# Attention scores and row maxima as products over one head's rows, and k and q placed early in an item

## The reference

```python
xn = _layernorm(x, axis=-1)
...
qkv = (x @ w_qkv.T + b_qkv).reshape(b, n, 3, H, D).transpose(2, 0, 3, 1, 4)
q, k, v = (qkv[0], qkv[1], qkv[2])
q = jax.nn.elu(q) + 1.0
k = jax.nn.elu(k) + 1.0
q = _apply_rope(q, sin, cos)
k = _apply_rope(k, sin, cos)
attn = jnp.einsum('bhnd,bhmd->bhnm', q, k) * scale
attn = jax.nn.softmax(attn, axis=-1)
attn_out = jnp.einsum('bhnm,bhmd->bhnd', attn, v)
...
x = x + s * g
```

## Time and profile before

| | us |
|---|---|
| three runs | 1500.83, 1501.16, 1502.19 |
| median | 1501.16 |
| span of the profiled execution | 1499.6 |
| PE busy | 1385.7 (92%) |
| VectorE busy | 1244.3 (83%) |
| ScalarE busy | 862.0 (57%) |
| GpSimd busy | 371.7 (25%) |
| 1024 score products (L1070), mean of one | 0.428 |
| 1024 maxima products (L1093), mean of one | 0.409 |
| 1024 reductions (L1217), mean of one | 0.685 |
| 1024 exponentials (L1154), mean of one | 0.600 |

### The profile page before, as it was taken

How to read it: one execution, slowest core, us unless ns; L and a number is a source line. 1 busy time by engine, 2 the same in 40 slices (tenths; PEclk the granted TensorE clock), 3 DMA queues, 4 the chain that set the end, 5 groups by cost and what they waited for, 6 DMA issues and landing times.

```text
span 1499.6 us, 25714 instructions
## 1 busy us (share of the span) xinstructions
PE 1385.7 (92%) x6898; PEld 875.8 (58%) x6898; DVE 1244.3 (83%) x2163; ACT 862.0 (57%) x1551; POOL 371.7 (25%) x455
## 2 busy tenths in 40 slices
PE   4599997999899894699999999999999999999998
PEld 4477775877677673455555555555555555555553
DVE  7799997999799995788887888888888888888881
ACT  5444453444345442057666766766766676676767
POOL 5012221221222315420330331232133033033000
PEclk8699999999999997599999999999999999999999
DMA  5211211112021111111011011101101101101100
GB/s 169 60 28 29 59 41 43 35 35 49 22 56 38 46 43 33 39 44 47 4 45 47 5 44 45 23 26 45 44 4 45 46 3 45 46 8 42 46 8 5
DMA packets 91576, 57.90 MB, mean 39 GB/s; under 512 B 38368, under 2 KB 85344, under 8 KB 90976
## 3 DMA queue, kind: packets, MB, share of 16 engines
q1 hardware_dynamic: 91488, 56.97, 15.1%
HBM read 29.04 MB, written 4.33 MB: 22 GB/s over the span
## 4 chain that ended last, share of the span: by engine, by line
PE 57%; DVE 2%; issue 1%; DMA 0%; ACT 0%; SPq 0%; ACTq 0%; POOLq 0%; POOL 0%; DVEq 0%
PE pa L1070 19%; PE pa L1082 17%; PE pa L1093 16%; PE pa L1116 2%; PE pa L1126 2%; PE pa L1121 1%; DVE neg_half L1217 1%; DVE feat L819 0%; ACT prob L1154 0%; PE pa L1110 0%; DVE w_cur L809 0%; DMA q_mask<-q_raw 0%; DMA w_all<-in_wqkv 0%; SPq L954 0%; SPq L965 0%
## 5 line engine op out<-in xcount | busy, mean ns | idle before, releaser
L1217 DVE TENSOR_REDUCE neg_half<-pa 128x1 f32<-128x512 f32 x1024 | 645.6, 685 | 128.3 <-PE pa L1093 115.2
L1154 ACT ACTIVATE prob<-pa 128x512 f32<-128x512 f32 x1024 | 545.1, 600 | 233.3 <-PE pa L1070 207.4
L1070 PE MATMUL pa<-q_sh,k_mask 128*128 128x512 f32 x1024 | 433.2, 428 | 4.9 <-ACT prob L1154 4.6
L1093 PE MATMUL pa<-k_raw,q_mask 128*128 128x512 f32 x1024 | 412.6, 409 | 1.3 <-DVE neg_half L1217 0.7
L559 ACT ACTIVATE hidden<-ps,b 128x512 f32<-128x512 f32 x320 | 220.5, 689 | 279.8 <-DVE hid_lo L591 187.9
L1070 PEld LDWEIGHTS pa<-q_sh,k_mask 128*128 128x128 f32 x1024 | 191.4, 188 | 240.7 <-ACT prob L1154 188.6
L591 DVE TENSOR_TENSOR hid_lo<-hidden,hid_hi 128x512 fp32r<-128x512 f32 x320 | 274.1, 857 | 10.9
L1082 PE MATMUL pa<-prob,v_st 128*32 128x512 f32 x2048 | 272.7, 604 | 1.1 <-ACT prob L1154 0.7
L1093 PEld LDWEIGHTS pa<-k_raw,q_mask 128*128 128x128 f32 x1024 | 196.2, 192 | 45.4 <-DVE neg_half L1217 18.0
L652 POOL TENSOR_TENSOR acc<-acc,gated 128x512 f32<-128x512 f32 x64 | 85.2, 1332 | 388.0 <-DVE gated L606 387.3
L589 DVE CAST hid_hi<-hidden 128x512 fp32r<-128x512 f32 x320 | 148.3, 463 | 35.8 <-ACT hidden L559 21.3
(11 more groups left out here) (136 smaller groups left out, 1065.4 us busy)
## 6 DMA issues: line engine op xcount, KB each, us to landing
gates<-gate_scratch SPq DMA_DIRECT2D x64, 256.0 KB, 4.9
k_mask<-k_raw SPq DMA_DIRECT2D x64, 128.0 KB, 2.6
q_sh<-q_raw SPq DMA_DIRECT2D x16, 512.0 KB, 3.1
q_mask<-q_raw SPq DMA_DIRECT2D x64, 96.0 KB
w_in<-in_w SPq DMA_DIRECT2D x4, 1280.0 KB, 6.2
x_q<-in_x SPq DMA_DIRECT2D x4, 512.0 KB, 7.2
x_c<-in_x SPq DMA_DIRECT2D x8, 256.0 KB, 5.5
rest_scratch<-rest SPq DMA_DIRECT2D x8, 256.0 KB, 5.4
```

What stands on the lines that cost most here:

```text
L1070: nc.tensor.matmul(score_bank(n, par, s)[:, :], k_mask[par][:, j, kt * P:(kt + 1) * P], q_sh[par][:, qh * CH:(qh + 1) * CH], start=True, s ...
L1093: nc.tensor.matmul(m_ps[(k + par) % MB][:, :], q_mask[par][:, j, qt * P:(qt + 1) * P], k_raw[par][:, kh * CH:(kh + 1) * CH], start=True, s ...
L1154: nc.scalar.activation(prob[s // J % 2][:, j, :], score_bank(n, par, s)[:, :], ACT.Exp, scale=SCALE)\
L1217: nc.vector.tensor_reduce(out=neg_half[par][:, qt, j, kh:kh + 1], in_=m_ps[(k + par) % MB][:, :], axis=AX.X, op=ALU.max, negate=True)\
```

## The change

- `k_mask`, `q_mask`, `q_sh`, their clearing, their DMAs and their semaphores are gone.
- A score product now takes rows 32j to 32j+26 of `k_raw` and `q_raw`, a maxima product rows 32j to 32j+24. The shift rows are placed into `q_raw`.
- The maxima go through the heads in another order (`part_of`), one step on, so that score and maxima of one slot have heads two apart.
- k and q of item n+1 are transposed in item n, in slots 3, 5, 9 and 11, instead of those of item n+2 in slots 47 to 61.
- The first eight rounds have a bank each.

```diff
-    AT_SHIFT1, AT_QKV, AT_K, AT_Q, AT_SHIFT0, AT_LAST_OUT = 23, (13, 17), (47, 51), (57, 61), 54, 7
+    AT_SHIFT1, AT_QKV, AT_K, AT_Q, AT_SHIFT0, AT_LAST_OUT = 23, (13, 17), (3, 5), (9, 11), 54, 7
...
+        def part_of(k):
+
+            return k // (2 * J), (k + 1) % J, k // J % 2
+
...
-            return psum[r] if type(n) is int and n == -2 else shared_ps
+            return psum[r] if type(r) is int and r < len(psum) else shared_ps
...
-            if f:
+            if m:
                 out += [(AT_K[h], "k", h) for h in range(2)] + [(AT_Q[h], "q", h) for h in range(2)]
...
-                    sp.dma_start(q_sh[par][rows, h * CH:(h + 1) * CH].bitcast(F32),
+                    sp.dma_start(q_raw[par][rows, h * CH:(h + 1) * CH].bitcast(F32),
...
-            for mask in (q_mask[0], k_mask[0]):
-                nc.gpsimd.memset(mask[:, :, :].bitcast(F32), 0.0).then_inc(mask_ok, 1)
...
-                nc.tensor.matmul(score_bank(n, par, s)[:, :], k_mask[par][:, j, kt * P:(kt + 1) * P],
-                                 q_sh[par][:, qh * CH:(qh + 1) * CH], start=True, stop=True).then_inc(s_full, 1)
+                rows = slice(j * ROWS, j * ROWS + SHIFT + 2)
+                nc.tensor.matmul(score_bank(n, par, s)[:, :], k_raw[par][rows, kt * P:(kt + 1) * P],
+                                 q_raw[par][rows, qh * CH:(qh + 1) * CH], start=True, stop=True).then_inc(s_full, 1)
...
-                nc.tensor.matmul(m_ps[(k + par) % MB][:, :], q_mask[par][:, j, qt * P:(qt + 1) * P],
-                                 k_raw[par][:, kh * CH:(kh + 1) * CH], start=True, stop=True).then_inc(max_full, 1)
+                rows = slice(j * ROWS, j * ROWS + SHIFT)
+                nc.tensor.matmul(m_ps[(k + par) % MB][:, :], q_raw[par][rows, qt * P:(qt + 1) * P],
+                                 k_raw[par][rows, kh * CH:(kh + 1) * CH], start=True, stop=True).then_inc(max_full, 1)
...
-                        if kind == "k" and has(n)[0]:
-
-                            act.wait_ge(max_full, HALVES * (n + 1))
-                            act.wait_ge(kmask_in[par], 16 * J * (n // 2 + 1))
-                        if kind == "q" and has(n)[0]:
-
-                            act.wait_ge(qmask_in[par], 16 * J * (n // 2 + 1))
-                            act.wait_ge(q_sh_in[par], 16 * (n // 2 + 1))
+                        if after(n):
+
+                            act.wait_ge(s_full, SLOTS * n)
```

More of the change, by code:

```diff
@@ L721, in attention @@
         q_raw = [sb(f"q_raw{i}", [P, T], F32R) for i in range(2)]
-        k_mask = [sb(f"k_mask{i}", [P, J, T], F32R) for i in range(2)]
-        q_mask = [sb(f"q_mask{i}", [P, J, T], F32R) for i in range(2)]
-        q_sh = [sb(f"q_sh{i}", [P, T], F32R) for i in range(2)]
         shift = [sb(f"shift{i}", [P, J, 2, CT], F32R) for i in range(2)]
@@ L756, in attention @@
         raw_ok = sem("a_raw_ok")
-        qmask_in = [sem(f"a_qmask_in{i}") for i in range(2)]
-        kmask_in = [sem(f"a_kmask_in{i}") for i in range(2)]
         max_full = sem("a_max_full")
@@ L765, in attention @@
         shift_in = [sem(f"a_shift_in{i}") for i in range(2)]
-        q_sh_in = [sem(f"a_q_sh_in{i}") for i in range(2)]
         v_st_ok = sem("a_v_st_ok")
@@ L923, in body @@
                       .then_inc(rest_in[par], 16)
[L924 to L936, removed]
                 if after(n):
@@ L943, in body @@
                     place_shift(n + 1, 1 - par, 0)
[L944 to L955, removed]
             def place_shift(m, par, h):
                 wait_apart(sp, shift_t_ok, 2 * m + h + 1, passed)
-                sp.wait_ge(q_sh_in[par], 16 * (m // 2 + 1))
                 for j in range(J):
@@ L1032, in body @@
                     operands(pool, nc.gpsimd, n + 2, par)
-                if type(n) is int and n == -1:
-                    for mask in (q_mask[1], k_mask[1]):
-                        nc.gpsimd.memset(mask[:, :, :].bitcast(F32), 0.0).then_inc(mask_ok, 1)
                 if after(n):
@@ L1086, in maxima @@
             def maxima(m, par, k):
[L1088 removed]
+                qt, j, kh = part_of(k)
                 if k == 0:
[L1090 removed]
                     pe.wait_ge(raw_ok, 4 * (m + 1))
                 pe.wait_ge(max_ok, HALVES * (m + 2) + turn(par, k))
[L1093 to L1094 removed]
+                rows = slice(j * ROWS, j * ROWS + SHIFT)
+                nc.tensor.matmul(m_ps[(k + par) % MB][:, :], q_raw[par][rows, qt * P:(qt + 1) * P],
+                                 k_raw[par][rows, kh * CH:(kh + 1) * CH], start=True, stop=True).then_inc(max_full, 1)
             def rounds(n, par, slot):
@@ L1101, in rounds @@
                     if kind in "kq":
-                        pe.wait_ge(front_ok, 3 * (n + 3))
+                        pe.wait_ge(front_ok, 3 * (n + 2))
                     if kind == "shift":
@@ L1106, in rounds @@
                         pe.wait_ge(pv_out, QH * (n - part) + part + 1 + 1)
-                    if not (type(n) is int and n == -2):
+                    if not (type(r) is int and r < len(psum)):
                         pe.wait_ge(round_free, r + 1)
@@ L1122, in rounds @@
                             continue
-                        st = stage[par]
+                        st = stage[1 - par]
                         heads = slice(J, 2 * J) if kind == "k" else slice(0, J)
@@ L1174, in rounds @@
                         act.wait_ge(round_full, r + 1)
-                        if kind == "k" and has(n)[0]:
-                            act.wait_ge(max_full, HALVES * (n + 1))
-                            act.wait_ge(kmask_in[par], 16 * J * (n // 2 + 1))
-                        if kind == "q" and has(n)[0]:
-                            act.wait_ge(qmask_in[par], 16 * J * (n // 2 + 1))
-                            act.wait_ge(q_sh_in[par], 16 * (n // 2 + 1))
-                        nc.scalar.activation({"k": k_raw, "q": q_raw}[kind][par][:, part * CH:(part + 1) * CH],
+                        if after(n):
+                            act.wait_ge(s_full, SLOTS * n)
+                        nc.scalar.activation({"k": k_raw, "q": q_raw}[kind][1 - par][:, part * CH:(part + 1) * CH],
                                              bank[:, :], ACT.Copy).then_inc(raw_ok, 1)
-                        act.wait_ge(raw_ok, 4 * (n + 2) + 2 * (kind == "q") + part + 1)
+                        act.wait_ge(raw_ok, 4 * (n + 1) + 2 * (kind == "q") + part + 1)
                         act.sem_inc(round_free, 1)
@@ L1214, in largest @@
             def largest(m, par, k):
-                qt, j, kh = k // 2 // J, k // 2 % J, k % 2
+                qt, j, kh = part_of(k)
                 dve.wait_ge(max_full, HALVES * m + k + 1)
```

3 lines of the change are left out of this document (removed).

## The result

| | us |
|---|---|
| after, five runs | 1827.4, 1785.21, 1789.65, 1790.75, 1777.26 |
| after, median | 1789.65 |
| before, five runs, median | 1501.16 (1500.4 to 1503.49) |
| ratio | 1.189, interval 1.186 to 1.192 |
| forecast | 1421, range 1375 to 1491 |

In the kernel's own runs the change makes it 19% slower; the forecast was 5% faster. The profiled execution is the one of 1827.4 (span 1825.4): with a mean granted clock of 0.66 against 0.68 to 0.69 in the other four it is 2% longer than they are, and it is the only one of the five with a profile.

What follows compares the result with a forecast made beforehand. PE was taken to bound the attention loop, VectorE next. Items falling from 54.07 to 49.5 us saved 68, item 15 1.4, the way in 10.8: 80.2 off 1499.6, adjusted to 1421 us, range 1375 to 1491.

Steps and rivals of the forecast that it cites:

- slower by the clock: Rival, 4%: PE stays at half clock with row-tiled products; group 3.9 us, item 68, total 1703 us.
- distance of neighbours in row tiles: Score and maxima products on PE: neighbours of different heads overlap, 0.1 us apart instead of 0.23.
- ordinary group: Attention loop, four slots and one value product without transposition rounds: 2.74 us instead of 3.05, VectorE pacing.
- item, k and q early, without the loop's edge: One attention item's sixteen groups: 24.7 for nine, 9.6 for three, 14.5 for four with the rounds.
- the four crowded groups: Slots 3 to 18 of an item, with seven rounds including early k and q: 14.5 us together.
- VectorE's busy share: Attention loop: VectorE busy for over 88%, where it was 83% before; a sign that the forecast is right.
- the loop's edge, every second item: Hardware loop's end: costs 1.5 us every second item, 0.75 an item, where it cost 0.97 before.
- way in, first maxima: Start of attention: without clearings and shared banks 10.8 us saved, first maxima at about 608.7 instead of 619.54.
- Weights one after another: Rival, 15%: each product waits for its own 0.19 us load; ordinary groups 2.87, item 51.7, total 1453 us.
- no overlap: Rival, 12%: products still go each 0.23 us, PE bounds as before, only the way in's 11 us remain: 1490.
- VectorE alone: Rival, 12%: VectorE's idle 0.34 us a group and the crowding vanish; item 45.5, total 1360 us.
- Slower by switching: Rival, 6%: changing product form costs 0.2 us more each way, 26 times an item; item 59.9, total 1577 us.

Runs made afterwards that it cites:

- 64-row kernels: Kernel before with score and maxima products over two heads' 64 rows, one head masked: 1445.32 us; with half-size masks, k and q late 1439.99, early 1459.35.
- 64 rows, early: Changed kernel (k and q in slots 3 to 11) with products over 64 rows and half-size masked copies: 1459.35 us, ratio 0.970.
- 64 rows, late: Kernel before (k and q late) with products over 64 rows and half-size masked copies: 1439.99 us, ratio 0.958.
- the first experiment: Kernel before with score and maxima products over one head's 26 or 24 rows, maxima's head order changed; masks and late k and q kept: 1634.63 and 1706.35 us.
- 128-row fillers: Changed kernel with four extra, overwritten score products over all 128 rows in each group: 1750.9 us.

## Why the prediction was wrong

**The step that failed** is none of the terms of the sum but the assumption under all of them, full clock in the loop. The prediction named the other case, slower by the clock, with the right mechanism and a group of 3.9, an item of 68 and 1703 us, and gave it 4%. Measured at half clock: a group of 4.20, an item of 76.5, 1790 us. The price was too low in both of its parts: the twelve other groups took 4.20 for the most part, not 3.9, and the four crowded ones 25.5 (1010.12 to 1035.59), where 68 less twelve groups of 3.9 leaves 21.

The 4% had no support. The trace of before showed no product on part of the rows, and at 620 us it showed PE at half clock with a product each 0.60. The prediction took this for a place of its own, and carried over the full clock of the loop to a loop in which each product would use a fifth of the rows. So the state of the clock, which was unknown, was treated as given, while the cost of each unknown operation was bounded with care. A range of 1375 to 1491 couldn't hold what a doubled cycle time gives.

**What held**, read at full clock, in the changed kernel's short stretches or in the 64-row kernels:

| step | forecast | measured | where |
|---|---|---|---|
| distance of neighbours in row tiles | 0.1 | 0.01, four at a time | after |
| ordinary group | 2.74 | 2.73 | after at full clock, 64 rows |
| item, k and q early, without the loop's edge | 48.8 | 50.7 | 64 rows, early |
| the four crowded groups | 14.5 | 15.5 | 64 rows, early |
| VectorE's busy share | over 88% | 88% (619.00 of 700 us) | 64 rows, late |
| the loop's edge, every second item | 1.5 | 1.3 (16.9 against 15.5 for the four groups after it) | 64 rows, early |
| PE's waits for DMAs in the loop | 0 | none of note | after |
| way in, first maxima | 608.7 | 608.61 | after |

The 88% answers VectorE's 83% of before: it is what paces these versions. The crowded groups were 1.0 too low, and with the rest of the item 1.9. For the changed kernel at full clock the early run gives an estimate: 1459.35, less the 3.0 by which its first maxima (611.65) is later than 608.61, near 1456, inside the range; no run shows that kernel, since the clock denies it.

Two of the exact hits are partly luck. In the group the maxima starts with the score (1289.56) and not 0.2 after it, but VectorE begins on it only 0.56 later (1290.12), where it was 0.44 before (652.69 to 653.13). On the way in, k and q are ready 9.6 sooner from the start of attention (9.3 forecast), and the first maxima follows them 2.3 sooner (1.5 forecast), but attention itself began 0.9 later in that execution (ScalarE's first instruction there at 588.29 instead of 587.35).

**The rivals.** Weights one after another and no overlap are refuted by four starts within 0.01, VectorE alone by the 2.73, since it needed groups near VectorE's own 2.4. Slower by switching didn't occur, since from the value product to the first score 1.00 passes (1288.56 to 1289.56), 0.99 before, and from the last maxima to the value product 0.42 (1290.87 to 1291.29), as the 0.43 where VectorE paced before; it was real where forms were mixed.

**What stays open.** The runs show which kernels had which clock, not what the chip measures. Why the first experiment gets full clock more often than the changed kernel and is 155 faster, why the 128-row fillers reach 0.94 and not 0.99, why products over 128 rows had half clock on the way in before, and whether data plays a part (the 64-row products stream a second head's data against zero weights) weren't told apart. A 32-row kernel with useful 128-row work among its products wasn't tried.

## What to carry to other kernels

Before counting on products over a part of the rows, treat the clock as one of the unknowns with a price, that of the whole loop at 1.2 GHz, and look at the granted clock first when the result comes. Use the largest tile that still allows the overlap needed: here two products side by side gave 4% (1440 against 1501), and four lost 19%. Don't mix 24-row products with 64- or 128-row ones as neighbours, and don't take PE's busy share as a sign that the clock is safe.

## What the hardware showed that I had not expected

- With products over 64 rows the granted clock was 0.99, with 24 and 26 rows 0.51 to 0.67, at a busy share of 95 to 96% each. But products over 128 rows, one each 0.60, had 0.50 as well on the way in of the kernel before.
- Extra products over 128 rows raised it from 0.51 to 0.94 and made the kernel 2% faster than without them (1751, a single run, against 1790). The same number over 26 rows left it at 0.50. The Trainium skill, TensorE: Matmul & The Clock Gate, Part 1, tells of the lower clock as the default and of activity as what releases it. In the run over 26 rows the busy share in the profile was 97% while the clock stayed at 0.50, so a high busy share there doesn't go with the full clock.
- Neighbours over 128 and 24 rows, or over 64 and 24, don't overlap at all, not even in loading weights, while neighbours over 26 and 24 start together: 0.72 from product to product at half clock, where products in one strip stand 0.43 apart, in two kernels (2666 and 2697 us).
- VectorE's TENSOR_SCALAR of 512 columns took 0.43 with no clearing beside it, 1.48 beside half-size clearings, and 6.60 beside full-size ones.
